# Layernorm by quarters, tiles mixed over pairs and two banks, ternary copies on VectorE

## The chip, the cores and the metric

One Trainium2 chip, one core. The metric is the device time in microseconds of one execution, the median of several runs. Engines are named TensorE (PE, with its weight loads as PEld), VectorE (DVE), ScalarE (ACT), GpSimd (POOL) and SyncE (SP, which here issues every transfer).

## What is computed

One transformer layer in fp32, on x of 8 batches x 1024 rows x 512. First differential attention: layernorm, q, k and v by one 512 x 1536 product, 16 heads of 32; the first 16 dimensions of a head give one softmax and the last 16 another; the second is subtracted with a factor; then a root-mean-square norm per head, and a product with wo. Then a feed-forward part with weights rounded to -1, 0, 1.

```python
qkv = x @ w_qkv                       # x is the layernorm of the input
a1 = softmax(einsum('bhsd,bhtd->bhst', q1, k1) * scale)
a2 = softmax(einsum('bhsd,bhtd->bhst', q2, k2) * scale)
out = einsum('bhst,bhtd->bhsd', a1 - lam * a2, v)
out_n = out / sqrt(mean(out * out) + EPS) * norm_w * (1.0 - LAMBDA_INIT)
x = x + (out_n reshaped) @ wo
h = bitlinear(ln(x), w_fc) + gate * (ln(x) @ v.T @ fast_b.T @ u.T)
x = x + bitlinear(relu(h) ** 2, w_proj)   # bitlinear: ternary weight times a row scale
```

## The kernel before, in words

**Chunks and tiles.** The 8192 rows are 16 chunks of 512 rows (C). A chunk of the input lies in `xin` as four row tiles of 128. Its layernorm is made in steps by `dve_ln_step`: four statistics (L1099), four gathers (L1104), a logarithm and an exponential on ScalarE (`act_ln`, L876 and L878), a correction step (`dve_newton`, L1110 to L1116) and four applies (`dve_apply`, L1121). Then it is turned: TensorE transposes it by column blocks of 128 (`pe_turn`, L479, four transposes each), ScalarE copies the result, rounded, to `xth` (`act_turn`, L884), and VectorE subtracts that for the low half `xtl` (`dve_turn`, L1148). From the turned rows come 12 tiles of a chunk (T, i = T mod 12): eight of q and k (i < 8), each of 12 matmuls (L503), with a copy on ScalarE (L900), a low half (`dve_low`, L1155) and a maximum of magnitudes (`dve_bound`, L1165) on VectorE, and three stores; and four of v (L506), with one ScalarE copy (L905) and no VectorE work.

**Pairs.** Chunks 0 and 1 (batch 0) are made ahead. Then 64 pairs of heads follow, eight in each batch. A pair has 16 slots (k), two in each of 8 steps (d = 0 to 7). A slot has two score halves on TensorE (`pe_score`, L564), two exponentials on ScalarE (`act_exp`, L921, 128x1024 each, 32 in a pair), one add of the probabilities into `acc` on VectorE (`dve_add`, L1222, 128x2048, none at slots 0 and 8), and the product with v (`pe_pv`, L589). The scores use banks 0 to 3, the products 4 and 5. `pe_sum` (L610) sums `acc` over partitions into bank 7, for slots 0 to 7 (j = 0) at step 5, and for 8 to 15 (j = 1) at step 1 of the next pair. ScalarE makes its reciprocal by a logarithm and an exponential (L927, L931).

What follows a pair X is spread over the next three (`*_posts`, d counts on from 8 and 16): combine (L1234, L1237), transpose (`pe_post` 3, L631), copy to `on` (L946), square on GpSimd (L283), sums (L1243), norm (L1248), split (L958, L1252), the product with wo into bank 7 (`pe_post` 14 and 15, L645), the residual on VectorE at d = 16 (L1258), and the store.

**The order** of each engine's instructions is written out by hand in loops over P, d and half; semaphores order the engines. In pair P the tiles 24 + 3P to 26 + 3P are made in pieces of 6, 8 or 4 matmuls at steps 0 to 5 (`PIECES`), all in bank 6: the first matmul of a tile waits, by `tile_read`, until the tile before has been read. Tiles come in the order of i: of four pairs, the first two make three q/k tiles, the third two and a v tile, the fourth three v tiles. All steps of a later chunk's layernorm lie in the first of four pairs and the start of the second (`steps`, `rest`); its four turns are at steps 2 and 6 of the second pair and at step 6 of the third and the fourth (`turn_at`). When the fourth pair's turn is done, SyncE loads the next chunk in one transfer. Pairs 0 to 51 carry layernorm and tiles, 52 to 55 tiles alone.

**The last eight pairs** have no tiles. There the weights are made ternary, one of eight tiles in each pair: magnitudes on ScalarE (L971), scale and comparison on VectorE (L1283 to L1298), four transposes of four blocks each on TensorE into bank 6 (`pe_ternary`, L732, at steps 6, 7, and 0, 1 of the next pair) and their copies on ScalarE (`act_ternary`, L982). In these pairs TensorE adds slots 7 and 15 itself (L618). Behind the loop come factors of the low-rank part, the rest of the last pairs, and the feed-forward part: 16 blocks of 512 rows (L669, L674, L689).

## Time and profile before

| what | us |
|---|---|
| median of 3 runs | 3943.78 (3939.89 to 3952.39) |
| profiled execution | 3940.3 |
| its span | 3938.6 |
| TensorE busy | 3774.7 (96%) |
| VectorE busy | 3205.4 (81%) |
| ScalarE busy | 2782.0 (71%) |
| GpSimd busy | 99.5 (3%) |
| mean granted clock of TensorE | 0.992 |

The span is the time from the first to the last instruction of the profiled execution. Busy time counts instructions in the engine and no waits. A granted clock of 1.00 is 2.4 GHz. In the trace, a wait is written with the one who waited ahead of the arrow and the one who ended it behind. A row of windows gives a stretch of the span, its length, then the busy time (and the number of instructions) of TensorE, its weight loads, VectorE, ScalarE and GpSimd, the granted clock, the share of the transfer engines' time, and GB/s. The stretches are cut at the first exponential (L921) of a pair. A group's row ends with its busy time in all, the mean of one in ns, and the idle time before it.

### The profile page before, as it was taken

The page shows a single profiled execution, that of the slowest core. Times are in us where ns is not written, and L with a number is a line of the kernel's source. Part 1 is how long each engine was busy: PE and PEld are TensorE (multiplying, and loading weights), DVE is VectorE, ACT ScalarE, POOL GpSimd, SP SyncE. Part 2 cuts the span into 40 slices and gives each one's busy share as a digit, 9 for nine tenths or more (in the row PEclk, how much of TensorE's full clock was granted, in tenths as well). Part 3 has the DMA queues.
Part 4 walks back from the last instruction along what each step waited for, and adds up shares of the span by engine and source line. Part 5 has one row for each costly group of instructions (what it writes and reads, how often), then busy time and mean ns, then how long its engine had stood idle before and what let it go on. Part 6 is the DMA issues. An engine that isn't in the chain of part 4 may idle for free.

```text
span 3938.6 us, 57545 instructions
## 1 busy us (share of the span) xinstructions
PE 3774.7 (96%) x21960; PEld 2070.1 (53%) x21960; DVE 3205.4 (81%) x3089; ACT 2782.0 (71%) x3597; POOL 99.5 (3%) x78
## 2 busy tenths in 40 slices
PE   6799999999999999999999999999889999999999
PEld 5344444444444444444444444333378888888887
DVE  5699999999999999999999999988855555555554
ACT  2688888888888888888888888988733333333333
POOL 0000000000000000000000000000000000000000
PEclk9899999999999999999999999999989999999999
DMA  5545444445444445444444445433101010101010
GB/s 196 129 101 114 99 112 108 102 107 111 111 99 114 108 96 121 104 108 104 108 106 107 112 93 115 103 74 90 48 10 43 22 43 22 43 22 43 22 43 22
DMA packets 225844, 338.24 MB, mean 86 GB/s; under 512 B 86704, under 2 KB 107184, under 8 KB 225008
## 3 DMA queue, kind: packets, MB, share of 16 engines
q1 hardware_dynamic: 225520, 333.88, 34.7%
q8 instruction: 208, 3.41, 0.4%
q14 instruction: 116, 0.95, 0.1%
HBM read 180.72 MB, written 150.99 MB: 84 GB/s over the span
## 4 chain that ended last, share of the span: by engine, by line
PE 65%; DVE 22%; ACT 5%; issue 5%; DMA 1%; SPq 1%; DVEq 0%; ACTq 0%
DVE acc L1222 17%; PE ps L589 13%; PE ps L689 12%; PE ps L669 12%; PE ps L564 10%; PE ps L506 5%; PE ps L645 4%; PE ps L503 3%; ACT pr L921 3%; PE ps L610 2%; PE ps L674 1%; DVE stg L1155 1%; PE ps L719 1%; DVE ot L1234 1%; PE ps L709 1%
## 5 line engine op out<-in xcount | busy, mean ns | idle before, releaser
L921 ACT ACTIVATE pr<-ps 128x1024 f32<-128x1024 f32 x2048 | 1989.7, 1032 | 278.4 <-PE ps L564 272.3
L1222 DVE TENSOR_TENSOR acc<-acc,pr 128x2048 f32<-128x2048 f32 x752 | 1736.5, 2309 | 39.5 <-ACT pr L921 16.0
L589 PE MATMUL ps<-pr,vst 128*32 128x512 f32 x8192 | 1023.3, 601 | 0.0
L564 PE MATMUL ps<-qst,kst 50*128 50x512 f32 x4096 | 800.0, 460 | 58.9 <-ACT pr L921 38.0
L564 PEld LDWEIGHTS ps<-qst,kst 50*128 50x128 f32 x4096 | 339.3, 184 | 730.8 <-ACT pr L921 515.5
L1075 ACT ACTIVATE rb<-ps,scf 128x512 f32<-128x512 f32 x256 | 176.7, 690 | 388.4 <-PE ps L674 388.4
L589 PEld LDWEIGHTS ps<-pr,vst 128*32 128x32 f32 x8192 | 208.5, 109 | 429.2 <-issue 423.8
L689 PE MATMUL ps<-tP,hh_ 128*128 128x512 f32 x1024 | 404.4, 395 | 1.9 <-DVE hl_ L1442 1.9
L669 PE MATMUL ps<-yh,tT 128*128 128x512 f32 x1024 | 404.5, 395 | 0.0
L669 PE MATMUL ps<-yl,tT 128*128 128x512 f32 x1024 | 399.5, 390 | 0.0
L689 PE MATMUL ps<-tP,hl_ 128*128 128x512 f32 x1024 | 399.1, 390 | 0.0
L1440 DVE TENSOR_TENSOR sb<-rb 128x512 f32<-128x512 f32 x256 | 176.9, 691 | 268.7 <-ACT rb L1075 267.1
L1222 DVE TENSOR_TENSOR acc<-pr 128x2048 f32<-128x2048 f32 x128 | 292.8, 2288 | 110.4 <-ACT pr L921 109.0
L1442 DVE TENSOR_TENSOR hl_<-sb,hh_ 128x512 fp32r<-128x512 f32 x256 | 177.3, 693 | 179.3 <-ACT hh_ L1080 179.3
L1080 ACT ACTIVATE hh_<-sb 128x512 fp32r<-128x512 f32 x256 | 162.4, 635 | 205.3 <-DVE sb L1440 205.3
L503 PE MATMUL ps<-xth,wqh 128*128 128x512 f32 x512 | 222.1, 434 | 31.3 <-DVE stg L1155 31.3
L689 PEld LDWEIGHTS ps<-tP,hh_ 128*128 128x128 f32 x1024 | 192.1, 188 | 56.8 <-DVE fo L1480 12.6
L669 PEld LDWEIGHTS ps<-yl,tT 128*128 128x128 f32 x1024 | 192.5, 188 | 38.9
L669 PEld LDWEIGHTS ps<-yh,tT 128*128 128x128 f32 x1024 | 192.5, 188 | 38.5
L689 PEld LDWEIGHTS ps<-tP,hl_ 128*128 128x128 f32 x1024 | 192.3, 188 | 37.7
L503 PE MATMUL ps<-xtl,wqh 128*128 128x512 f32 x512 | 206.7, 404 | 0.0
L503 PE MATMUL ps<-xth,wql 128*128 128x512 f32 x512 | 202.3, 395 | 0.0
(154 smaller groups left out, 3493.6 us busy)
## 6 DMA issues: line engine op xcount, KB each, us to landing
qst<-q_scratch SPq DMA_DIRECT2D x128, 384.0 KB, 6.3
kst<-k_scratch SPq DMA_DIRECT2D x128, 384.0 KB, 9.6
q_scratch<-stg SPq DMA_DIRECT2D x168, 256.0 KB
k_scratch<-stg SPq DMA_DIRECT2D x168, 256.0 KB
xin<-in_L_attn_x_dram SPq DMA_DIRECT2D x16, 1024.0 KB, 5.4
v_scratch<-vsg SPq DMA_DIRECT2D x64, 256.0 KB, 3.1
vst<-v_scratch SPq DMA_DIRECT2D x128, 128.0 KB, 5.4
xr<-in_L_attn_x_dram SPq DMA_DIRECT2D x64, 256.0 KB
```

Of the source, the lines that this page charges most:

```text
L503: t = e.matmul(ps[:, bk, :], w[:, k, m0:m0 + 128], xx[:, k, :], start=(n == 0), stop=(n == 11))
L506: t = e.matmul(ps[:, bk, :], xx[:, k, st * 128:(st + 1) * 128], w[:, k, 2 * E:3 * E], start=(n == 0), stop=(n == 11))
L564: ins = e.matmul(ps[:, 2 * c + hh, :], kst[rows, r, j, t * 128:(t + 1) * 128], qst[rows, r, j, c * 512:(c + 1) * 512], start=True, stop=True)
L589: ins = e.matmul(ps[32 * c4:32 * c4 + 32, 4 + j, :], vst[:, r, t, 32 * hh:32 * hh + 32], pr[:, sl, c, hh, :], start=(t == 0), stop=(t == 7 ...
L669: e.matmul(ps[:, bk, :], tT[:, k, i * 128:(i + 1) * 128], y_[:, bf, k, :], start=(m == 0), stop=False)
L689: t = e.matmul(ps[:, rt, :], h_[:, uu % 3, rt * 128:(rt + 1) * 128], tP[:, i, :], start=(i == 0 and part == 0), stop=(i == 15 and part == 1))
L921: e.activation(pr[:, sl, c, :, :], ps[:, 2 * c:2 * c + 2, :], ACT.Exp, scale=SCALE).then_inc(s_exp, 1)
L1075: e.activation(rb[:, uu % 2, :], ps[:, 4 + uu % 2, :], ACT.Relu, scale=scf[:, 0, i:i + 1]) \
L1080: e.activation(hh_[:, uu % 3, :], sb2[:, uu % 2, :], ACT.Copy).then_inc(s_hh, 1)
L1222: e.tensor_tensor(acc[:, j, :], old, new, ALU.add).then_inc(s_add, 1)
L1440: e.tensor_tensor(sb2[:, uu % 2, :], rb[:, uu % 2, :], rb[:, uu % 2, :], ALU.mult).then_inc(s_sb, 1)
L1442: e.tensor_tensor(hl_[:, uu % 3, :], sb2[:, uu % 2, :], hh_[:, uu % 3, :], ALU.subtract) \
```

## The change

- The layernorm of chunks 3 to 15 goes by quarters. Pair P works for chunk C = P // 4 + 3 and row tile st = P mod 4 (`part_of`). VectorE takes one statistic in each pair at step 0 (all four of chunk 3 in pair 0), gathers them in the first of four pairs at step 1 and corrects at step 3. The apply becomes a ScalarE instruction with a scale and a bias per row, one in each pair at step 5. TensorE transposes the four blocks of that row tile at step 6 (`pe_part`), with one copy and one subtraction behind it. Each pair loads one row tile of the next chunk.
- Tiles follow `ORDER`: in an even chunk each pair has two q/k tiles and one v tile, in an odd one the pairs have 2, 3, 3 and 0 q/k tiles. The second tile of each pair goes to bank 7, the others to bank 6 (`TILE_BANK`); the waits follow.
- The square of a pair's result is a ScalarE instruction out of bank 5 (step 4) instead of a GpSimd one.
- The residual (L1258 of before) comes half a step earlier, ahead of the last add.
- The ternary transposes are at steps 0, 2, 3, 4 of the next pair (`TERNARY`), and their copies on VectorE; the last tile's four lie behind the loop.

```diff
+TILE_BANK = (6, 7, 6)
+ORDER = ((0, 1, 8, 2, 3, 9, 4, 5, 10, 6, 7, 11), (0, 1, 8, 2, 3, 4, 5, 6, 7, 9, 10, 11))
+TERNARY = (0, 2, 3, 4)
...
 def turned(P):
-    return min(12 + P // 4 * 4 + (0, 0, 2, 3)[P % 4], 4 * NC)
...
+    return min(12 + P, 4 * NC)
...
-            for X in range(NPAIR):
...
-                e.wait_ge(s_raw, X + 1)
-                if X:
-                    e.wait_ge(s_ssq, X)
-                e.tensor_tensor(sq[:], on[:], on[:], ALU.mult).then_inc(s_osq, 1)
...
+        def sync_part(e, P):
+
+            C, st = part_of(P)
+            e.wait_ge(s_xt, turned(P) + 1)
+            e.dma_start(xin[:, st, :], x_chunk(C + 1)[:, st, :]).then_inc(s_xp[st], 16)
...
-                    if d == 7 and P % 4 == 3 and w + 4 < NC:
-                        sync_x(e, w + 4)
+                    if d == 7 and w + 4 < NC:
+                        sync_part(e, P)
...
+        def pe_part(e, P):
+
+            C, st = part_of(P)
+            e.wait_ge(s_pap, P + 1)
+            e.wait_ge(s_pt, 2 * P + 1)
+            for k in range(4):
+                t = e.transpose(ps[:, 4, k * 128:(k + 1) * 128], xin[:, st, k * 128:(k + 1) * 128], ident[:])
+            t.then_inc(s_xt, 1)
...
                 if j == 0:
                     e.wait_ge(s_xtl, turned(P))
                 elif P:
-                    e.wait_ge(s_raw, P)
+                    e.wait_ge(s_osq, P)
...
                 e.wait_ge(s_rln, 2 * X)
-                e.wait_ge(s_flv, 6 * min((X + 1) // NP + 1, B) - 1)
+                if 3 * X + 24 < 24 * B:
+                    tile_read(e, 3 * X + 25)
...
-                            if T > 24:
+
+                            if a == 1:
+                                e.wait_ge(s_rln, 2 * P)
+                                e.wait_ge(s_flv, 5)
+                                e.wait_ge(s_xtl, 12)
+                            elif a == 2:
+                                tile_read(e, T - 2)
+                                if q == NP - 1:
+                                    e.wait_ge(s_flv, 6 * (P // NP + 1) + 5)
+                            elif P:
                                 tile_read(e, T - 1)
                             else:
                                 e.wait_ge(s_xtl, 12)
-                        pe_tile(e, T, 6, n0, n1)
+                        pe_tile(e, T, TILE_BANK[a], n0, n1)
...
-                    if turn_at(P, d):
-
-                        e.wait_ge(s_pt, 2 * P + (1 if d == 6 else 0))
-                        pe_turn(e, *turn_at(P, d))
+                    if d == 6 and part_of(P):
+                        pe_part(e, P)
                     pe_posts(e, P, d)
-                    if last and d >= 6:
-                        pe_ternary(e, P - (NPAIR - NP), d - 6)
-                    if last and d < 2 and P > NPAIR - NP:
-                        pe_ternary(e, P - (NPAIR - NP) - 1, d + 2)
+                    if P > NPAIR - NP and d in TERNARY:
+                        pe_ternary(e, P - (NPAIR - NP) - 1, TERNARY.index(d))
...
-            pe_pv(e, NSLOT - 2)
-            pe_ternary(e, 7, 2)
-            pe_pv(e, NSLOT - 1)
-            pe_ternary(e, 7, 3)
+            for m in range(4):
+                if m in (0, 2):
+                    pe_pv(e, NSLOT - 2 + m // 2)
+                pe_ternary(e, 7, m)
...
+        def act_part_apply(e, P):
+            st = P % 4
+            e.wait_ge(s_pnv, 9 * (P // 4) + 9)
+            e.activation(xin[:, st, :], xin[:, st, :], ACT.Identity, bias=ln_t[:, 20 + st:21 + st],
+                         scale=rs[:, 8 + st:9 + st]).then_inc(s_pap, 1)
...
+            if d == 4 and half == 1:
+                if X:
+                    e.wait_ge(s_ssq, X)
+                e.activation(sq[:], ps[:, 5, :], ACT.Square).then_inc(s_osq, 1)
...
-                    if P % 4 == 0 and d == 6 and w + 3 < NC:
-                        act_ln(e, w + 3, mv, ln_t, rs)
+                    if d == 2 and P % 4 == 0 and part_of(P):
+                        act_part_ln(e, w)
...
-                        act_tile(e, 24 + 3 * P + d // 2, 6)
-                    if turn_at(P, d):
-                        act_turn(e, *turn_at(P, d))
+                        act_tile(e, 24 + 3 * P + d // 2, TILE_BANK[d // 2])
+                    if d == 5 and part_of(P):
+                        act_part_apply(e, P)
+                    if d == 6 and part_of(P):
+                        act_part(e, P)
...
-                    if d >= 6 and tile >= 0:
-                        act_ternary(e, tile, d - 6)
-                    if d < 2 and tile >= 1:
-                        act_ternary(e, tile - 1, d + 2)
...
-            if d == 16 and half == 0:
+            if d == 15 and half == 2:
...
-            steps = {(1, 1): (0,), (2, 0): (1,), (3, 0): (2,), (4, 0): (3,), (5, 0): (4,), (6, 1): (6,), (7, 0): (7,),
-                     (7, 1): (8,)}
-            rest = {(0, 0): (9,), (0, 1): (10,)}
...
+                        if (d, half) == (0, 1) and P < 4 * (NC - 3) - 3:
+                            dve_part_stats(e, P)
+                        if P % 4 == 0 and part_of(P):
+                            if (d, half) == (1, 0):
+                                dve_part_gather(e, w)
+                            if (d, half) == (3, 1):
+                                dve_part_newton(e, w)
...
+                        if d == 7 and half == 1:
+                            dve_post(e, P - 2, 15, 2)
                         dve_add(e, P, 2 * d + half)
+                        if tile >= 1 and d in TERNARY and half == 1:
+                            dve_turn_ternary(e, tile - 1, TERNARY.index(d))
...
-            dve_post(e, NPAIR - 3, 16, 0)
+            for m in range(4):
+                dve_turn_ternary(e, 7, m)
```

## Rows read from the trace of the kernel before

**Rows 1.** Windows of the run: pairs 0 to 51, 52 to 55, 56 to 63.

```profile
130.10:2331.20 2201.10, 2149.26 (x13700) 953.17 (x13702) 2094.95 (x1585) 1894.30 (x2307) 82.87 (x51) 1.00 0.46 106
2331.20:2495.80 164.60, 163.77 (x1051) 71.84 (x1040) 156.24 (x107) 143.66 (x173) 5.35 (x4) 1.00 0.49 113
2495.80:2838.70 342.90, 309.96 (x2041) 107.52 (x2038) 301.46 (x264) 302.34 (x415) 8.92 (x10) 1.00 0.33 73
```

**Rows 2.** Windows by pair: 20, 21, 22 and 23, then 8 and 12.

```profile
976.05:1018.50 42.45, 40.77 (x264) 17.98 (x260) 41.25 (x41) 36.24 (x47) 2.09 (x1) 1.00 0.48 113
1018.50:1062.15 43.65, 41.86 (x272) 18.83 (x268) 42.90 (x33) 36.86 (x46) 1.04 (x1) 1.00 0.46 110
1062.15:1103.75 41.60, 41.35 (x268) 18.32 (x264) 40.54 (x27) 36.39 (x45) 1.04 (x1) 1.00 0.45 103
1103.75:1145.20 41.45, 41.45 (x272) 18.42 (x268) 37.05 (x29) 36.49 (x46) 2.26 (x1) 1.00 0.46 103
467.70:511.70 44.00, 42.34 (x264) 18.28 (x260) 41.57 (x41) 36.24 (x46) 2.08 (x1) 0.96 0.47 109
638.10:680.70 42.60, 40.94 (x264) 17.98 (x260) 41.37 (x41) 36.36 (x47) 2.07 (x1) 1.00 0.48 113
```

**Rows 3.** Waits in pair 20, pair 21 (two) and pair 22: us in total, times, longest.

```profile
PE ps L503 <- DVE stg L1155: 1.7, 1, 1.7
...
PE ps L610 <- DVE xr L1258: 1.0, 1, 1.0
PE ps L503 <- DVE stg L1155: 0.8, 2, 0.4
...
ACT pr L921 <- PE ps L564: 4.9, 9, 0.8
```

**Rows 4.** Groups of the whole run; then single lines with ns min/median/max.

```profile
L1222 DVE TENSOR_TENSOR acc<-acc,pr 128x2048 f32<-128x2048 f32 x752 | 1736.5, 2309 | 39.5 <-ACT pr L921 16.0 <-DVE acc L1222 1.0
L1075 ACT ACTIVATE rb<-ps,scf 128x512 f32<-128x512 f32 x256 | 176.7, 690 | 388.4 <-PE ps L674 388.4
L931 ACT ACTIVATE rl<-rl 128x512 f32<-128x512 f32 x128 | 81.2, 634 | 4.1
L1155 DVE TENSOR_TENSOR stg<-ps,stg 128x512 fp32r<-128x512 f32 x112 | 76.5, 683 | 0.0
L1472 DVE CAST zt<-ps 32x512 fp32r<-32x512 f32 x16 | 11.1, 697 | 0.5
...
L1222 DVE TENSOR_TENSOR acc<-acc,pr x752: 2215/2286/2903, 138.7 to 2837.2; 128x2048 f32<-128x2048 f32 x188
...
L283 POOL TENSOR_TENSOR sq<-on x64: 1038/1041/3062, 194.5 to 2862.3; 128x512 f32<-128x512 f32 x64
...
L1099 DVE BATCH_NORM_STATS2 st<-xin x64: 675/684/694, 9.9 to 2189.4; 128x6 f32<-128x512 f32 x64
L1121 DVE TENSOR_SCALAR xin<-xin,mv,rs x64: 529/540/547, 26.3 to 2211.3; 128x512 f32<-128x512 f32 x64
...
L982 ACT ACTIVATE tP<-ps x16: 580/600/628, 2702.2 to 2842.1; 128x512 fp32r<-128x512 f32 x16
```

**Rows 5.** Pair 58: its window, and waits in it.

```profile
2580.70:2623.70 43.00, 38.95 (x260) 13.56 (x256) 37.22 (x31) 37.89 (x53) 1.04 (x1) 1.00 0.36 81
...
DVE acc L1222 <- ACT pr L921: 3.4, 2, 3.2
ACT tT L982 <- PE ps L732: 2.8, 2, 1.8
ACT rl L927 <- PE ps L618: 2.0, 2, 1.5
```

**Rows 6.** Transfers; VectorE's timeline behind the loop; ScalarE's at the start.

```profile
xin<-in_L_attn_x_dram SPq DMA_DIRECT2D x16, 1024.0 KB, 5.4
...
2855.58 0.75 DVE L1258 SCALAR_TENSOR_TENSOR xr<-ps,nw,xr 128x512 f32<-128x512 f32 x1 [5.40 <-DMA xr<-in_L_attn_x_dram]
...
0.80 1.28 ACT L1001 ACT_TABLE_LOAD   x1 [0.80 <-PEq L1506]
```

More of the change, by code:

```diff
@@ L209, in build @@
         s_lnv, s_lna = sem("s_lnv"), sem("s_lna")
+        s_pst, s_pnv, s_pap, s_pta = (sem(n) for n in ("s_pst", "s_pnv", "s_pap", "s_pta"))
+        s_xp = [sem(f"s_xp{k}") for k in range(4)]
         s_xt, s_xth, s_xtl, s_tile, s_qh, s_ql, s_qx, s_v, s_flv, s_flp = (
@@ L496, in pe_tile @@
                 k, part = divmod(n, 3)
-                if i == 0 and part == 0:
+                if i == 0 and part == 0 and C < 3:
                     e.wait_ge(s_xtl, 4 * C + k + 1)
+                elif i == 0 and n == 0:
+                    e.wait_ge(s_xtl, 4 * C + 4)
                 w = (wqh, wql, wqh)[part]
@@ L610, in pe_sum @@
                     t = e.matmul(ps[32 * c4:32 * c4 + 32, bk, :], ones[:], acc[:, j, (2 * c + hh) * 512:(2 * c + hh + 1) * 512],
[L611 to L612 removed]
+                                 start=True, stop=not pe_adds(X, j), skip_group_check=True)
+            if pe_adds(X, j):
                 gg = 16 * X + 8 * j + 7
@@ L1370, in vector_program @@
                     for half in range(2):
-                        if half == 1 and turn_at(P, d):
-                            dve_turn(e, *turn_at(P, d))
+                        if (d, half) == (6, 1) and part_of(P):
+                            dve_turn_part(e, P)
                         if d == 5 and half == 0:
```

171 lines of the change are left out of this document (103 added, 68 removed).

## The prediction, made before the changed kernel was built or run

> **What bounds the kernel now.** I read the stages first, cut at the first exponential of pairs 0, 52, 56 and behind 63 [rows 1]: 52 pairs that still make q, k and v tiles take 2201.1 us (42.33 each), four that make tiles but have no layernorm left take 164.6 (41.15 each), the last eight, which turn ternary weights instead, 342.9 (42.9 each). The feed-forward part behind them is not touched. In the first stage TensorE is busy 2149.3 of 2201.1 us: it is the bound, and 51.8 us are gaps. Next, one group of four pairs [rows 2]: 42.45, 43.65, 41.60 and 41.45 us, TensorE busy in 40.77, 41.86, 41.35 and 41.45 of them. So a pair with one turn of rows (268 matmuls) needs 41.35 us; one with none (264) 0.6 less, one with two (272) 0.5 more. The gaps, 3.7 us in four pairs, lie in the first two, where VectorE is fullest (41.25 and 42.90 us; 37.05 in the fourth). Then who ends the gaps [rows 3]: a q or k tile's first matmul waits 1.7 and 0.8 us for L1155, VectorE's low half of the tile before, because every tile uses bank 6, and the row sums L610 wait 1.0 us for L1258, which empties bank 7. VectorE is late there, not full on average: it is busy 161.74 of 169.15 us.
>
> A second thing comes on top of such gaps: pair 8 takes 44.0 us at a granted clock of 0.96, pair 12, with the same work, 42.6 at 1.00 [rows 2]. At the halved clock (1.2 GHz instead of 2.4) stands a short stretch of the slow pair. I count four of these (pairs 4, 8, 36 and 40, about 1.5 us each, 6 us together), all in a pair that begins with the 1.7 us gap.
>
> The last eight pairs are another case: in pair 58 [rows 5] ScalarE is busy 37.89 us and waits 2.8 us for L732, the ternary transposes, and 2.0 for the row sums: 42.7 of 43.0. It is the bound; TensorE needs 38.95, VectorE 37.22.
>
> **The change, part by part**, against the profiled execution: 3940.3 us, of which the span is 3938.6; the median of the three runs, 3943.8, is 3.5 above it.
>
> Layernorm. Four applies (L1121, 0.540 us each) leave VectorE per four pairs, one small instruction comes, so 2.0 us less per four pairs. The four statistics, 0.684 each, stay, but lie one in each pair instead of four in the first. ScalarE gets one apply per pair with a scale and a bias from memory. No row shows that form. SBUF to SBUF without pointers takes 0.634 us (L931); a pointer scale adds 0.09 (L1075, 0.690, beside 0.600 of L982, both out of PSUM) [rows 4]. I take 0.81 with two pointers, between 0.63 and 0.90. For this the trace has a contrary number: it was 0.54 on VectorE. In a sentence of its own: the Trainium skill, "ScalarE: Activation LUTs", Rules for kernel authors, tells to do adds and multiplies on VectorE, not on ScalarE; by that rule the step is a loss of 0.27 us of engine time per apply, which would count only if ScalarE were the bound, and that is the third rival.
>
> Squares. GpSimd's product (L283, 1.04 us alone, up to 3.06) becomes a ScalarE instruction out of PSUM, 0.60 us by L982. VectorE gains what the overlap cost it: the 752 long adds average 2.309 us where the median is 2.286 [rows 4], 17 us in all, 0.27 a pair. In sentences of their own: the Trainium skill, "SBUF — State Buffer", Who interferes with whom, says that the pair of ports which the two engines share is locked and the loser waits in full; each product would then cost VectorE up to 1.04 us, 66 us in all, and removing it would be worth four times as much. The median and the mean above show that most products cost nothing, and I keep 17.
>
> So VectorE's load in four pairs goes from 161.7 to 161.7 - 2.0 - 1.1 = 158.6 us, 39.7 a pair against 41.35 of TensorE.
>
> Tiles. In groups with an even chunk every pair now has two q/k tiles, each with L1155 (0.68 us) and a reduction of the same length, and one v tile, which needs no VectorE; in the odd groups the counts are 2, 3, 3, 0. The middle tile goes to bank 7, between the row sums of j = 1 and those of j = 0, so the third tile waits for the first, two steps back, not for the one before. This takes away the place of the 1.7 and 0.8 us waits. L1258 moves half a step earlier, in front of the last add; both stand ahead of the row sums either way, so only the lighter VectorE helps there. The nearest rows for the new state are pairs 52 to 55: three q/k tiles, one bank, no layernorm, and gaps of 164.6 - 163.8 = 0.8 us in four pairs [rows 1]. The new plain pair has as many VectorE instructions (two tiles, a statistic and a subtraction of a turn instead of a third tile), the first of each group has nine small ones more, the odd groups' middle pairs two long ones more. I leave 12 us of VectorE gaps in 52 pairs (0.2 each as there; bounds 0 and half of the present 52).
>
> ScalarE. Per pair it gets 0.60 (square, step 4) and 0.81 (apply, step 5), 1.41 beside 36.4 busy of 42. In pair 22 it waits for scores nine times, 4.9 us, 0.8 at most [rows 3]. The square finds such a wait just behind it; the apply stands behind a logarithm, an exponential and a tile copy, where there is none, and its 0.81 must go into the waits of the next step, of which some 0.6 is free. I take 0.2 us a pair on the path, 10 us; the bounds are 0 and all of the 1.41, 73 us.
>
> DMA. SyncE issues 52 loads of 256 KB instead of 13 of 1 MB. A load starts when TensorE has turned its quarter at step 6, behind the v load on the queue, and the statistic that needs it comes at step 0 of the next pair, two steps (some 10 us) later; 1 MB lands in 5.4 us [rows 6], so I cost it at nothing. Were this cover gone, VectorE would stand in order for up to 5 us a pair with its adds behind. The transposes of a quarter at step 6 wait for the apply of step 5 and free bank 4 as before; their count is the same.
>
> First stage: 51.8 - 12 - 10 = 30 us, plus 5 of the 6 us of halved clock, because the gap ahead of those stretches goes: **35 us** less.
>
> Ternary copies. From ScalarE go four copies (2.4 us) and the 2.8 us of waits for their transposes, and 0.6 comes: 38.3 us. VectorE gets four copies out of PSUM, 0.697 by L1472 [rows 4]: 37.2 + 2.8 = 40.0, and of its 3.4 us of waits for exponentials [rows 5] at least 0.8 stays: 40.8. So VectorE becomes the bound: 2.2 us less in seven pairs, 0.5 in pair 56, **16 us** (bounds: 0 where TensorE's transposes wait for late copies, and 28 at 39.4 us a pair, TensorE's need with half a microsecond of gap).
>
> End. Two more ternary pieces lie behind the loop, each a transpose and a copy in turn, about 1.5 us. They hide beneath two transfers, after which L1258 waits another 5.40 us [rows 6]. Without that cover 3 us; I take **1 us** more.
>
> Sum: 3940.3 - 35 - 16 + 1 = 3890 us. Another execution may lie a few microseconds to either side, as the median of before does; I add nothing for it.
>
> **The rivals.** (a) Everything at TensorE's floor: gaps and dips nearly all gone (54 us) and 39.7 us in the last pairs (26): 3860. For it: pair 23 has no gap at all. Against: no ScalarE room at step 5. (b) The waits move on to the row sums and to late exponentials, a third of the first stage's gain and 5 us at the end stay: 3940 - 15 - 5 = 3920. For it: L610 already waits for L1258 [rows 3]. (c) Slower: ScalarE becomes the path at steps 4 and 5. Its waits are short ones between scores; if none takes the 1.41 us, every exponential behind it, and with it the score and the add that wait for it, comes that much later, the present gaps stay, and only the 16 us of the end are won: 3940 + 73 - 16 = 3997. It decides once more than about 1.2 us a pair is on the path (35 + 10 + 16 over 52). (d) The new functions need another table than the one loaded at the start. The trace shows one such load, 1.28 us [rows 6]; there and back once a pair would be 2.6 us in 64 pairs: 3890 + 164 = 4054. The Trainium skill, "ScalarE: Activation LUTs", Table sets, says that the cheap functions are filler in every set; its examples have identity, not square. That the change doesn't do what it says is a variant of (b): the stages keep their order, and only the load moves.
>
> **How the numbers follow.** Forecast, 3872 to 3908, 0.62; (a) 0.14; (b) 0.15; (c) 0.06; (d) 0.03. The range leaves out (c), (d) and the far parts of (a) and (b): 3860 to 3925. What a measurement here tells from no change is 0.3%, 12 us; (b) reaches into that a little. Faster 0.88, same 0.04, slower 0.08.
>
> **What would show it.** Right: pairs 0 to 51 near 41.7 us with hardly a wait on L1155's counterpart; no short stretches at half clock inside them; last pairs near 40.8 with VectorE above 39.5 and ScalarE waiting for scores; long adds with mean equal to median. Wrong: first-stage pairs still above 42; exponentials 11 to 13 of each pair late with TensorE idle ahead of a score; table loads inside the pairs; VectorE idle for a quarter's load at the start of a pair.

## The result, and the profile after

The changed kernel takes 3922.69 us (median of five runs, 3919.04 to 3923.53), the kernel before 3943.78 (3938.83 to 3952.39): a ratio of 0.9942 (0.9927 to 0.9958). That is faster by 21 us, where 50 had been forecast: the right side, inside the outer range (3860 to 3925) but outside the forecast's own (3872 to 3908), and less than half of the size. The profiled execution after took 3922.69 us, its span 3920.9. Against the span of before that is 17.7 us, and the rest of this text accounts for them.

Windows of the kernel after, cut at the same first exponentials as in [rows 1]: pairs 0 to 51, 52 to 55, 56 to 63, and what lies behind. Columns: length, then busy time of TensorE, its weight loads, VectorE, ScalarE and GpSimd, then the granted clock, the DMA share and GB/s.

```profile
131.50:2304.10 2172.60, 2152.33 (x13700) 954.40 (x13702) 2067.74 (x1542) 1946.65 (x2411) 0.00 (x0) 1.00 0.47 108
2304.10:2467.50 163.40, 163.40 (x1048) 71.92 (x1040) 154.39 (x107) 144.98 (x177) 0.67 (x2) 1.00 0.48 114
2467.50:2818.30 350.80, 309.50 (x2032) 105.19 (x2030) 311.15 (x292) 293.30 (x393) 0.00 (x0) 0.99 0.32 71
2818.30:3920.90 1102.60, 1080.16 (x4852) 877.48 (x4844) 594.63 (x1026) 408.69 (x654) 0.20 (x1) 0.99 0.10 32
```

| us | up to pair 0 | 0 to 51 | 52 to 55 | 56 to 63 | behind | span |
|---|---|---|---|---|---|---|
| before | 130.1 | 2201.1 | 164.6 | 342.9 | 1099.9 | 3938.6 |
| after | 131.5 | 2172.6 | 163.4 | 350.8 | 1102.6 | 3920.9 |
| difference | +1.4 | -28.5 | -1.2 | +7.9 | +2.7 | -17.7 |
| forecast | 0 | -35 | 0 | -16 | +1 | -50 |

The forecast is off by 32 us of span. Of these 24 are in the last eight pairs, which became 7.9 us longer instead of 16 shorter, and 6.5 in the first stage. The 1.4 us ahead of pair 0 mean nothing: that stretch takes 129.9 to 131.9 us in the kernels of this text. The 1.2 us in pairs 52 to 55 go with the second bank: the kernels with one bank take 164.4 there (experiments 5 and 10), the others 163.4 to 163.5. Nothing in the last eight pairs was slowed by more work on a full engine. VectorE is busy 311.15 of 350.80 us, ScalarE 293.30, TensorE 309.50; all three have more than 39 us to spare.

Windows by pair after: 20, 21, 22, 23 (their counterparts are the first four of [rows 2]), and pair 58 (before: [rows 5]).

```profile
966.97:1009.14 42.17, 41.62 (x268) 18.35 (x264) 40.60 (x37) 37.78 (x49) 0.00 (x0) 1.00 0.46 108
1009.14:1050.74 41.60, 41.37 (x268) 18.45 (x264) 39.97 (x30) 37.40 (x47) 0.00 (x0) 1.00 0.53 122
1050.74:1092.39 41.65, 41.43 (x268) 18.45 (x264) 40.75 (x30) 37.40 (x48) 0.00 (x0) 1.00 0.51 121
1092.39:1134.27 41.88, 41.66 (x272) 18.48 (x268) 38.82 (x30) 37.50 (x48) 0.00 (x0) 1.00 0.41 84
2552.23:2596.02 43.79, 38.47 (x260) 13.27 (x256) 38.69 (x35) 36.60 (x50) 0.00 (x0) 1.00 0.35 80
```

The four pairs of a group are nearly level now: 42.17, 41.60, 41.65 and 41.88 where they had been 42.45, 43.65, 41.60 and 41.45. The 1.7 and 0.8 us waits for a tile's low half [rows 3] are gone. In pairs 3 to 51 there is no stretch at half clock any more, where there were four. Near the start of the stage one is left, in pair 1; before, it was in pair 2. The groups that answer to [rows 4], ns per instruction behind the comma:

```profile
L1296 DVE TENSOR_TENSOR acc<-acc,pr 128x2048 f32<-128x2048 f32 x752 | 1719.9, 2287 | 50.3 <-ACT pr L965 18.6
...
L919 ACT ACTIVATE xin<-xin,ln_t,rs 128x512 f32<-128x512 f32 x52 | 42.3, 813 | 0.0
...
L994 ACT ACTIVATE sq<-ps 128x512 f32<-128x512 f32 x64 | 39.0, 609 | 0.0
...
L751 PE MATMUL ps<-ident,tt 128*128 128x128 f32 x128 | 21.5, 293 | 15.9 <-DVE tP L1384 9.1 <-DVE tT L1384 6.8
...
L1384 DVE CAST tT<-ps 128x512 fp32r<-128x512 f32 x16 | 10.9, 684 | 0.0
```

Every duration of the prediction holds: the long adds mean 2287 ns where 2286 was the median before, the apply takes 813 ns (0.81), the square 609 (0.60), the copy on VectorE 684 (0.697). What was wrong lies in how they join, and the fourth row shows it: TensorE's ternary transposes (L751) now wait 15.9 us for the copies, 12.5 of them in pairs 57 to 63 and the rest behind the loop.

Pair 58 after, the longest waits and then its timeline from 12.3 us into the pair (start, duration, engine, line; in brackets the idle time before it and what ended that):

```profile
ACT pr L965 <- PE ps L583: 6.9, 6, 1.9
DVE acc L1296 <- ACT pr L965: 4.0, 3, 2.1
...
ACT rl L971 <- PE ps L638: 2.0, 2, 1.0
PE ps L751 <- DVE tT L1384: 1.7, 1, 1.7
```

```profile
2564.51 7.08 DVE L1296 TENSOR_TENSOR acc<-acc,pr 128x2048 f32<-128x2048 f32 x3
...
2569.98 0.66 PE L650 MATMUL ps<-ident,ot 128*128 128x128 f32 x4
...
2571.51 0.69 DVE L1384 CAST tT<-ps 128x512 fp32r<-128x512 f32 x1
...
2572.34 0.63 PE L751 MATMUL ps<-ident,tt 128*128 128x128 f32 x4 [1.70 <-DVE tT L1384]
...
2573.44 1.94 ACT L965 ACTIVATE pr<-ps 128x1024 f32<-128x1024 f32 x2 [1.89 <-PE ps L583]
```

Read it from below. ScalarE stands idle 1.89 us for a score; the score is behind the third piece's transposes (L751) on TensorE; these need bank 6, which the copy of the second piece (L1384) empties; and that copy is on VectorE behind three adds in a row, 7.08 us. The same chain is in each of the seven pairs 57 to 63; TensorE's wait is 1.70 us in six of them and 2.30 in pair 62. Three pairs lose more behind it, in a stretch where TensorE is at half its clock: pairs 57, 58, 60 and 63 take 43.8 to 43.9 us, pair 59 takes 44.7, pair 61 44.6 and pair 62, with its longer wait, 45.3. One such stretch, in pair 59:

```profile
2617.00:2620.40 3.40, 3.40 (x16) 0.81 (x14) 3.33 (x9) 2.43 (x3) 0.00 (x0) 0.53 0.02 5
```

The longer wait, in pair 62:

```profile
2749.79 0.97 PE L751 MATMUL ps<-ident,tt 128*128 128x128 f32 x4 [2.30 <-DVE tP L1384]
```

In the stretch of pair 59 eight products of probabilities take 1.93 us, where eight take 1.06 elsewhere in these pairs.

### The profile page after: what moved, and what is told of

It is laid out like the page before. It is cut to its first block, busy times and chain, and to the rows that moved or that the text cites. A ratio compares the mean times of both kernels' runs of the same rounds, so it can differ in the third digit from the quotient of the medians.

```text
span 3920.9 us, 57542 instructions
## 1 busy us (share of the span) xinstructions
PE 3780.6 (96%) x21960; PEld 2070.3 (53%) x21960; DVE 3191.6 (81%) x3082; ACT 2824.7 (72%) x3681; POOL 2.0 (0%) x14
## 4 chain that ended last, share of the span: by engine, by line
PE 77%; ACT 9%; DVE 8%; issue 4%; SPq 1%; DMA 1%; DVEq 0%; ACTq 0%
PE ps L608 17%; PE ps L583 13%; PE ps L708 12%; PE ps L688 12%; PE ps L521 8%; DVE acc L1296 6%; ACT pr L965 5%; PE ps L664 5%; PE ps L630 3%; PE ps L524 3%; PE ps L693 1%; ACT rl L971 1%; ACT rl L975 1%; ACT xin L919 1%; PE ps L738 1%
## 5 line engine op out<-in xcount | busy, mean ns | idle before, releaser
L965 ACT ACTIVATE pr<-ps 128x1024 f32<-128x1024 f32 x2048 | 1982.0, 1030 | 265.5 <-PE ps L583 259.5
L1296 DVE TENSOR_TENSOR acc<-acc,pr 128x2048 f32<-128x2048 f32 x752 | 1719.9, 2287 | 50.3 <-ACT pr L965 18.6
L583 PE MATMUL ps<-qst,kst 50*128 50x512 f32 x4096 | 809.5, 462 | 65.5 <-ACT pr L965 44.6
```

What stands on the lines that cost most here:

```text
L583: ins = e.matmul(ps[:, 2 * c + hh, :], kst[rows, r, j, t * 128:(t + 1) * 128], qst[rows, r, j, c * 512:(c + 1) * 512], start=True, stop=True)
L965: e.activation(pr[:, sl, c, :, :], ps[:, 2 * c:2 * c + 2, :], ACT.Exp, scale=SCALE).then_inc(s_exp, 1)
L1296: e.tensor_tensor(acc[:, j, :], old, new, ALU.add).then_inc(s_add, 1)
```

## The experiments

Two questions: why the last pairs became longer, and what the parts of the first stage are worth. Each kernel is the changed one with the edit shown, if nothing else is said. Stages are from each kernel's profile, ratios against the kernel before on the same chip.

How far a stage repeats can be read from kernels whose code in pairs 0 to 51 is the same: the changed one and experiments 1, 2 and 11 take 2172.6, 2170.4, 2174.0 and 2172.5 us there. All of that scatter is in the first four pairs, where none, one or two stretches at half clock come. Pairs 4 to 51 have none in any kernel but the one before, so they are the better measure for small effects (worked out from the starts of the pairs' first exponentials):

| us | pairs 0 to 3 | stretches there | pairs 4 to 51 |
|---|---|---|---|
| before | 167.0 | 1 | 2034.2 (with four stretches) |
| after | 167.0 | 1 | 2005.6 |
| 1, 2, 11 | 164.8, 168.6, 166.9 | 0, 2, 1 | 2005.6, 2005.4, 2005.6 |
| 3: square on GpSimd | 168.6 | 2 | 2008.7 |
| 4: apply on VectorE | 164.0 | 0 | 1982.9 |
| 5: one bank | 165.5 | 0 | 2018.1 |
| 6: unmixed | 166.8 | 1 | 2005.9 |
| 8 | 163.7 | 0 | 1983.0 |
| 9: correction late | 166.0 | 1 | 1976.4 |
| 10: spreading alone | 166.1 | 1 | 2006.4 |

The windows of pairs 4 to 51 before, after and in experiment 4:

```profile
297.05:2331.23 2034.18, 1989.35 (x12700) 883.73 (x12696) 1942.94 (x1477) 1751.52 (x2137) 76.63 (x48) 1.00 0.46 107
298.47:2304.08 2005.61, 1990.33 (x12700) 884.49 (x12696) 1917.25 (x1438) 1800.45 (x2234) 0.00 (x0) 1.00 0.47 108
294.73:2277.59 1982.86, 1978.50 (x12700) 882.31 (x12696) 1926.90 (x1486) 1767.35 (x2186) 0.00 (x0) 1.00 0.48 110
```

**1. The end as before.** Places, bank and engine of the ternary copies as in the kernel before; the rest of the change stays.

```diff
-                    if P > NPAIR - NP and d in TERNARY:
-                        pe_ternary(e, P - (NPAIR - NP) - 1, TERNARY.index(d))
+                    if last and d >= 6:
+                        pe_ternary(e, P - (NPAIR - NP), d - 6)
+                    if last and d < 2 and P > NPAIR - NP:
+                        pe_ternary(e, P - (NPAIR - NP) - 1, d + 2)
...
+                    if d >= 6 and tile >= 0:
+                        act_ternary(e, tile, d - 6)
+                    if d < 2 and tile >= 1:
+                        act_ternary(e, tile - 1, d + 2)
```

> The changed kernel with the ternary transposes and copies put back: transposes at steps 6, 7, 0, 1, copies on ScalarE. Theory A (the last eight pairs were never bound by ScalarE's load: the 2.8 us that it waited for the ternary transposes were TensorE's queue, and the new order adds a wait of 1.7 us for a copy behind VectorE's adds): last eight pairs 346 us (343 of before plus 0.5 a pair for the square), against 350.8 changed; whole 3917. Theory B (ScalarE's load was the bound there, and something else, such as the square, costs the gain): moving 2.4 us a pair back to ScalarE makes the last eight pairs longer, 360 or more; whole 3932.

Measured 3909.82 us, ratio 0.9918 (0.99 to 0.9935). The last eight pairs are back at their length, what lies behind them takes 1100.0 us, and no stretch at half clock is left in the pairs:

```profile
2464.40:2807.00 342.60, 309.99 (x2038) 107.77 (x2038) 296.12 (x264) 305.78 (x423) 0.00 (x0) 1.00 0.33 73
```

So this part of the change costs 8.2 us in the pairs and 2.6 behind them; in pairs 0 to 3 this execution is 2.2 us shorter besides, with no stretch at half clock there. Theory B falls. It also says that the square, 0.6 us on ScalarE in each of these pairs, costs nothing here, where 0.5 had been expected: 342.6 with it and 342.9 without.

**2. The third piece in bank 7.** Places and engine as in the change; only the bank of one piece in four differs, so that its transposes do not wait for the second piece's copy.

```diff
+def ternary_bank(i, m):
+    return 7 if i < 7 and m == 2 else 6
...
-            if u4:
+            if i < 7 and m == 2:
+                e.wait_ge(s_rln, 2 * (NPAIR - NP + i + 1))
+            elif i < 7 and m == 3:
+                e.wait_ge(s_tt, u4 - 1)
+            elif u4:
```

> The changed kernel with the third ternary transpose of a tile in bank 7, so that it does not wait for the copy of the second. Theory A (one wait for a bank): the 1.7 us wait at step 3 goes in seven pairs (12 us), and with it the three short stretches of halved clock behind it (2.5 us): last eight pairs 336 us, whole 3908. Theory C (VectorE's load, not the bank, holds the last pairs): the wait moves to the next place that needs VectorE, last eight pairs 347 or more, whole 3919 or more.

Measured 3903.86 us, ratio 0.99 (0.9883 to 0.9918). Windows of pair 58 and of the last eight pairs, then pair 58's longest waits of ScalarE:

```profile
2550.83:2592.72 41.89, 38.26 (x260) 13.31 (x256) 38.69 (x35) 36.61 (x51) 0.00 (x0) 1.00 0.37 84
2468.00:2802.30 334.30, 304.40 (x2034) 104.81 (x2030) 310.92 (x292) 292.81 (x393) 0.00 (x0) 1.00 0.33 75
```

```profile
ACT pr L975 <- PE ps L587: 5.0, 5, 1.8
...
ACT rl L981 <- PE ps L644: 2.0, 2, 1.0
```

One bank is worth 16.5 us: 350.8 becomes 334.3. Seven pairs have 41.9 to 42.0 us each, the wait of 1.70 us (2.30 in pair 62) is gone in all of them, and with it the three stretches at half clock. Without that wait this part of the change, new places and copies on VectorE together, gives 8.3 us against experiment 1 (342.6), half of the 16 forecast.

**3. The square back on GpSimd.**

```diff
+                e.wait_ge(s_raw, X + 1)
+                if X:
+                    e.wait_ge(s_ssq, X)
+                e.tensor_tensor(sq[:], on[:], on[:], ALU.mult).then_inc(s_osq, 1)
...
-                e.activation(sq[:], ps[:, 5, :], ACT.Square).then_inc(s_osq, 1)
```

> The changed kernel with the square back on GpSimd. Theory A: in pairs 0 to 51 the square falls into a wait of ScalarE and costs nothing, in the last eight it costs 0.5 us each: pairs 0 to 51 within 3 us of 2172.6, last eight 347, whole 3919; long adds of VectorE at a mean of 2.31 again. Theory D (every ScalarE instruction in steps 4 to 6 is on the path): 0.6 us less in each of 60 pairs, whole 3887.

Measured 3925.32 us, ratio 0.9958 (0.9943 to 0.9974), the first stage 2177.3 us against 2172.6, the last pairs 349.9.

```profile
L1301 DVE TENSOR_TENSOR acc<-acc,pr 128x2048 f32<-128x2048 f32 x752 | 1739.4, 2313 | 43.7 <-ACT pr L974 7.2
...
L293 POOL TENSOR_TENSOR sq<-on 128x512 f32<-128x512 f32 x64 | 80.1, 1252 | 2727.5 <-ACT on L999 2727.5
```

The long adds are back at 2313 ns, 26 more than after, or 19.5 us of VectorE's time in the run. Of the 4.7 us in the first stage 3.1 are in pairs 4 to 51, nearly all of them in the first pair of each group (42.4 us against 42.2); the rest is in pairs 0 to 3, with one more stretch at half clock. The last pairs are 0.9 us shorter because two of them have such a stretch and not three; without one they take 43.8 us as after. So ScalarE's path is no shorter without the square, and theory D falls. The whole is 2.6 us above the changed kernel, and the runs of the two overlap.

**4. The apply back on VectorE**, still one quarter a pair, right ahead of the add of step 4's second half.

```diff
-                    if d == 5 and part_of(P):
-                        act_part_apply(e, P)
...
+                        if (d, half) == (4, 1) and part_of(P):
+                            dve_part_apply(e, P)
```

> The changed kernel with the quarter's apply on VectorE (0.54 us, one in each pair, at step 4) instead of ScalarE. Theory A (ScalarE has no room at step 5; VectorE has 1.5 us a pair to spare): step 5 about 0.7 us shorter, step 6 0.3 longer, 0.4 us less in each of 52 pairs, 20 us in all: pairs 0 to 51 2152 us, whole 3902. Theory E (VectorE's late adds hold the row sums as soon as anything is added): the 0.54 us come back as waits of the row sums at step 5, pairs 0 to 51 2170 us or more, whole 3920 or more.

Measured 3898.23 us, ratio 0.9892 (0.9872 to 0.9912). The first stage, and pair 21:

```profile
130.80:2277.60 2146.80, 2137.15 (x13700) 951.84 (x13702) 2078.15 (x1594) 1911.03 (x2359) 0.00 (x0) 1.00 0.48 109
997.25:1038.37 41.12, 41.12 (x268) 18.42 (x264) 40.29 (x31) 36.70 (x46) 0.00 (x0) 1.00 0.51 123
```

25.8 us less in 52 pairs, and 22.7 in pairs 4 to 51, 0.47 each (the other 3.0 us are in pairs 0 to 3, where this execution has no stretch at half clock and the changed kernel's has one). ScalarE had been busy only 37.4 of 41.6 us, and still 0.5 of the 0.81 us lay on the path. Only this place on ScalarE was tried: whether the apply would have been free at another step of it is open. Look at TensorE too: the same 268 matmuls are busy 41.12 us here and 41.37 after, so half of the loss hid inside TensorE's busy time.

**5. All tiles in bank 6**, the row sums alone in bank 7.

```diff
-TILE_BANK = (6, 7, 6)
+TILE_BANK = (6, 6, 6)
```

> The changed kernel with all q, k and v tiles in bank 6 again (order of the tiles, layernorm by quarters and the last pairs as changed). Theory A (the second bank takes away a wait for the low half wherever a q or k tile follows one): about 0.3 to 0.5 us of gap in most of pairs 0 to 51, these 2190 us, whole 3940 beside 3922.7. Rival F (spreading layernorm and tiles already lets VectorE be in time, the bank gives nothing): pairs 0 to 51 within 3 us of 2172.6.

Measured 3936.45 us, ratio 0.9986 (0.9976 to 0.9996). The first stage, and from the waits of pair 9 those for the low half L1220:

```profile
130.70:2314.35 2183.65, 2149.63 (x13700) 951.92 (x13702) 2067.60 (x1542) 1951.20 (x2410) 0.00 (x0) 1.00 0.46 107
```

```profile
PEld ps L524 <- DVE stg L1220: 0.7, 1, 0.7
PEld ps L521 <- DVE stg L1220: 0.4, 1, 0.4
...
PE ps L524 <- DVE stg L1220: 0.3, 1, 0.3
```

The second bank is worth 11.1 us of the first stage, 12.5 in pairs 4 to 51, somewhat less than the 17 expected: TensorE's wait that comes back is 0.3 us (0.7 for its weight load), not the 1.7 of [rows 3]. That fits VectorE's work being spread now; it was not tried apart. (This kernel's profiled run, 3932.88 us, is the shortest of its ten.)

**6. Tiles not mixed**: eight q and k tiles, then four v tiles, over the two banks.

```diff
-ORDER = ((0, 1, 8, 2, 3, 9, 4, 5, 10, 6, 7, 11), (0, 1, 8, 2, 3, 4, 5, 6, 7, 9, 10, 11))
+ORDER = (tuple(range(12)), tuple(range(12)))
```

> The changed kernel with the tiles of a chunk in their old order (3, 3, 2, 0 q/k tiles in four pairs), two banks kept. Theory A (with two banks only the row sums wait for VectorE, and layernorm is spread): the first of each four pairs about 0.5 us longer, the rest as changed, pairs 0 to 51 2180 us, whole 3930. Rival G (the mix of tiles is what removed the gaps): pairs 0 to 51 2195 us or more, whole 3945.

Measured 3920.74 us, ratio 0.9951 (0.9934 to 0.9968), the first stage 2172.63 us against 2172.60, and pairs 4 to 51 2005.9 against 2005.6. With two banks the mix gives nothing. The expectation of a loss falls.

**7. Edits 2 and 4 together.**

> The third ternary transpose in bank 7 and the apply on VectorE together. Theory A (the two costs lie in different stages and add): pairs 0 to 51 2147 us, last eight 334, whole about 3880. Rival H (the second gain is limited by something that the first left): less than 35 us of gain over the changed kernel, whole 3888 or more.

Measured 3880.3 us, ratio 0.9845 (0.9823 to 0.9867): the first stage 2148.8, the last pairs 334.4. The two gains add up, as they should if they lie in different stages.

**8. Besides, the last tile's four copies alternate between banks 6 and 4** behind the loop, where the change has bank 6 four times in turn.

```diff
+    if i == 7:
+        return 4 if m % 2 else 6
```

> As the one before, and the four transposes behind the loop alternate between banks 6 and 4. Theory A (the end is longer by 2.8 us since those transposes and copies take turns, and the product behind them then runs at half the clock): the stretch behind pair 63 comes back to 1100 us or a little less, whole 3 us less than the one before. Rival I (two transfers in a row set that stretch, as before): no difference within 1 us.

Measured 3877.8 us, ratio 0.9843 (0.9821 to 0.9865). What lies behind the loop is 1101.1 us against 1102.9 in experiment 7: 1.8 less, and in the medians not to be told from nothing.

**9. Besides, the small instructions of the layernorm** in the first pair of a group half a step later: behind the add that the row sums of step 5 wait for, not ahead of it.

```diff
+                        if (d, half) == (4, 0) and P % 4 == 0 and part_of(P):
+                            dve_part_newton(e, w)
...
-                            if (d, half) == (3, 1):
-                                dve_part_newton(e, w)
```

> As x8 (third ternary transpose in bank 7, apply on VectorE, two banks behind the loop), with the correction of the layernorm in the first of four pairs half a step later, behind the add of slot 7 instead of in front of it. Theory A (the first of four pairs is 0.5 us longer because the row sums at step 5 wait for that add): 41.2 instead of 41.7 us in 13 pairs, pairs 0 to 51 2140 us, whole 3872. Rival J (the 0.5 us is something else of that pair, such as ScalarE's logarithm and exponential at step 2): no difference beyond 1 us.

Measured 3874.08 us, ratio 0.9838 (0.9824 to 0.9852), the fastest here. Its first stage, pair 20 (the first of its group), and its last pairs:

```profile
130.75:2273.20 2142.45, 2137.55 (x13700) 949.72 (x13702) 2076.65 (x1594) 1911.64 (x2358) 0.00 (x0) 1.00 0.47 109
955.60:996.72 41.12, 41.12 (x268) 18.37 (x264) 39.97 (x38) 37.10 (x49) 0.00 (x0) 1.00 0.50 111
2436.60:2770.90 334.30, 304.24 (x2030) 104.57 (x2030) 310.76 (x292) 292.93 (x393) 0.00 (x0) 1.00 0.34 74
```

The first pair of a group now takes 41.12 us with TensorE busy in all of it, and the stage 4.3 us less than in experiment 8 (2146.8), close to what was expected. In pairs 4 to 51 it is 6.6 us, 0.55 in each of twelve groups; a stretch at half clock in pair 1, which experiment 8 does not have, hides the rest. The whole first stage is shorter than TensorE's busy time in it before (2149.26 [rows 1], some of it at half clock).

**10. The spreading alone**: statistics, apply and load by quarters, the apply on VectorE; the square on GpSimd, one bank, tiles unmixed and the end as before.

> Only the spreading of layernorm over the pairs is left of the change: apply on VectorE, square on GpSimd, one bank, old order of tiles, last eight pairs as before. Theory A (the parts add up: spreading alone takes away some 40 of the 51.8 us of gaps, the second bank another 11, and the apply on ScalarE gave 26 back): pairs 0 to 51 2160 us, last eight 343, whole 3900. Rival K (spreading needs the lighter VectorE of the other parts): pairs 0 to 51 2175 us or more, whole 3915 or more.

Measured 3912.79 us, ratio 0.9934 (0.9918 to 0.995), the first stage:

```profile
129.86:2302.34 2172.48, 2144.74 (x13700) 946.13 (x13702) 2107.77 (x1594) 1892.47 (x2308) 69.93 (x51) 1.00 0.47 108
```

This lies between the two expectations and nearer to the second, that the banks and the square have a share of their own. The spreading alone takes 28.6 us off the first stage of before, just what the whole change takes off. The second bank, the square and the mix together take another 25.7 (the first stage of experiment 4 is this plus those three), and the apply on ScalarE gives the same 25.8 back; in pairs 4 to 51 the two are 23.5 and 22.7. Taken out one by one of the changed kernel the same three are worth 12.5, 3.1 and 0.2 there (experiments 5, 3 and 6), 15.8 together: they are worth more beside an apply on VectorE. No run shows why. The median, 3912.79 us, is likewise below the 3922.69 of the whole change. One pair of the last eight took 44.1 us in this run, with a stretch at half clock in it; the pairs beside it took 42.9 to 43.1, and the reading does not rest on it.

**11. The copies on VectorE, everything else of the end as before**: the old steps 6, 7, 0 and 1, each copy ahead of the add of its half step.

```diff
+                        if tile >= 0 and d >= 6 and half == 1:
+                            dve_turn_ternary(e, tile, d - 6)
+                        if tile >= 1 and d < 2 and half == 1:
+                            dve_turn_ternary(e, tile - 1, d + 2)
```

> The ternary transposes at their old steps (6, 7, 0, 1) as in x1, but their copies on VectorE, ahead of the add of the same half step. So ScalarE loses 2.4 us a pair and TensorE's order does not change. Theory A (at steps 6 and 7 ScalarE waits for a score that TensorE has queued behind the product with wo and the transpose; the wait only changes the instruction that it is written on): steps 6 and 7 stay at 6.0 us, only step 0 may lose up to 0.5: last eight pairs 339 to 343 us. Theory B, the one of the prediction (ScalarE is the bound in these pairs, its waits for the transposes go with the copies): 2.4 to 5.2 us less a pair, last eight pairs 326 us or less.

Measured 3913.86 us, ratio 0.9928 (0.9908 to 0.9947); the last eight pairs take 345.9 us, 3.3 more than in experiment 1, where ScalarE copies in the same places. That is the test of the step on which the 16 us had stood: theory B is off by 20 us, and theory A, right in kind, by 3 (its range ended at 343). ScalarE's waits in pair 58 with the copies on ScalarE (experiment 1):

```profile
ACT tT L1032 <- PE ps L751: 2.8, 2, 1.8
ACT rl L973 <- PE ps L638: 1.5, 2, 1.0
ACT pr L967 <- PE ps L583: 0.2, 1, 0.2
```

and with the copies on VectorE (experiment 11), with the pair's window ahead:

```profile
2551.21:2594.64 43.43, 38.78 (x260) 13.48 (x256) 38.78 (x35) 36.58 (x50) 0.00 (x0) 1.00 0.36 81
```

```profile
ACT pr L967 <- PE ps L583: 6.9, 6, 2.2
...
ACT rl L973 <- PE ps L638: 2.1, 2, 1.0
```

The 2.8 us of waits for the transposes are gone by name only. ScalarE does 1.7 us less (36.58, and 38.27 in experiment 1), and its exponentials wait 6.9 us for scores instead of 0.2. Pair 58's window in experiment 1:

```profile
2549.20:2592.10 42.90, 38.88 (x260) 13.58 (x256) 36.35 (x31) 38.27 (x54) 0.00 (x0) 1.00 0.36 82
```

## Why the prediction was wrong, and where it was right

Steps of pair 58, from the first exponential of each step to that of the next, worked out from the starts of L965 or its counterpart (a tile's four pieces lie at steps 6, 7, 0 and 1 in the first three kernels, at 0, 2, 3 and 4 in the last two):

```
us                                    0     1     2     3     4     5     6     7    pair
before                              5.23  5.93  4.23  4.85  4.09  6.54  6.07  6.04  43.0
1: end as before                    5.22  5.93  4.22  4.84  4.57  6.07  6.05  6.04  42.9
11: old places, copies on VectorE   5.50  5.93  4.57  4.84  4.57  6.03  6.00  6.00  43.4
after                               4.75  5.92  4.57  6.89  4.57  5.98  5.56  5.56  43.8
2: third piece in bank 7            4.75  5.91  4.57  5.00  4.57  5.99  5.55  5.55  41.9
```

**The step that failed: "From ScalarE go four copies (2.4 us) and the 2.8 us of waits for their transposes ... So VectorE becomes the bound: 2.2 us less in seven pairs".** It read a full engine out of busy time plus waits: 37.89 busy, 2.8 and 2.0 of waits, 42.7 of 43.0 [rows 5]. Two things were wrong with that. (VectorE's load came out lower too, 38.69 us where 40.0 had been summed: the copies added 2.3 us to it, and without the product on GpSimd its small instructions took 0.9 less. ScalarE's 38.3 are 38.1 by the terms given.)

First, a wait is not work that leaves with the instruction that waits. The two waits of before, 1.05 us in step 6 and 1.78 in step 7, were for TensorE's queue: at these steps the product with wo stands in it ahead of the transposes and ahead of the next scores. With the copies gone from ScalarE, the exponential behind them waits instead, 1.48 and 2.22 us in experiment 11, and still 1.03 and 1.78 after, where no transposes are left in steps 6 and 7 at all. In the table the columns 6 and 7 fall by 0.05 us at most when the copies change their engine, and by half a microsecond each when the transposes leave TensorE's queue there. The Trainium skill, "PSUM — Partial Sum Buffer", Engine vs sequencer instructions, says that matmuls start and complete in program order; so a wait for a matmul lasts until what stands ahead of it in the queue is done. The table agrees. Columns 6 and 7 together give 0.9 us a pair for the new places of the pieces (experiment 2 against 11); the copies on VectorE in the old places give nothing and cost 3.3 us (experiment 11 against 1). The fourth combination, new places with the copies on ScalarE, was not run, so how much of the 8.3 us needs VectorE is open.

Second, the change put the second and third pieces into neighbouring steps with one bank, and their copy onto an engine that has up to three adds of 2.29 us ahead of it. Column 3 is where it shows: 6.89 us against 5.00 with another bank. The prediction had this as its lower bound ("0 where TensorE's transposes wait for late copies"); it lay at zero, and measured it was +8, for it took the wait to eat a gain and not to stand beside a gain that was not there. Worked out: 1.9 us in seven pairs are 13.2, the longer wait of pair 62 is 0.6 and the three stretches at half clock behind these waits some 2.6, 16.4 together, of the 16.5 that the bank gives back in experiment 2.

Without the wait the term is 8.3 us (experiments 1 and 2), not 16: the pair stands at 41.9, not 40.8. Which engine holds it there was not tried; VectorE is busy 38.69 of 41.89 us and ScalarE 36.61, so neither is full.

**The end, +1 forecast, +2.7 measured.** Right in kind. Behind the loop four transposes and four copies take turns in one bank. VectorE's timeline there, and one row of TensorE's:

```profile
2823.24 0.69 DVE L1384 CAST tP<-ps 128x512 fp32r<-128x512 f32 x1 [1.27 <-PE ps L751]
2825.70 0.69 DVE L1384 CAST tP<-ps 128x512 fp32r<-128x512 f32 x1 [1.76 <-PE ps L751]
...
2835.75 0.42 DVE L1496 COPY ut<-ps 128x256 f32<-128x256 f32 x1 [5.69 <-PE ps L638]
...
2838.37 0.74 DVE L1332 SCALAR_TENSOR_TENSOR xr<-ps,nw,xr 128x512 f32<-128x512 f32 x1
```

```profile
2822.12 1.08 PE L751 MATMUL ps<-ident,tt 128*128 128x128 f32 x4 [2.47 <-DVE tP L1384]
```

The cover named was the transfer for which the residual behind the loop waited 5.40 us [rows 6]. Its counterpart, L1332, now waits for nothing and starts 20.1 us behind the end of the last exponential, where it was 16.9, and VectorE waits 5.69 us for TensorE instead: the cover was used up, and TensorE's chain of transposes, wo product and sums became the path. Seven of the wo product's twelve matmuls take 0.63 us or more, at half clock; before, all but the first took 0.39 or 0.40.

**The first stage, 35 forecast, 28.5 measured.** The mechanism was right, the sizes were not, and that the total came near is in part luck: the apply cost 16 us more than its term, and the other two terms came out 10 better:

| term, us | forecast | measured | by |
|---|---|---|---|
| the stage without the two below | 2149.3 - 5 = 2144.3 | 2142.5 | experiment 9 |
| ScalarE's apply on the path | 10 | 25.8 | experiment 4 |
| VectorE's gaps left | 12 | 4.3 | experiments 8 and 9 |
| sum | 2166.3 | 2172.6 | |

In pairs 4 to 51, free of stretches at half clock in these kernels, the apply costs 22.7 us and the gaps are 6.6: the apply was taken at less than half, whichever is used.

- The apply. Its duration was right (0.81 forecast, 813 ns measured) and so was its place: "a logarithm, an exponential and a tile copy" ahead of it, and no wait. Step 5 of pair 22 takes 6.38 us after and 5.69 in experiment 4; step 6 gives back 0.31 (4.97 and 5.28), and step 7 loses 0.13 again. "Of which some 0.6 is free" was the mis-sized part: half of that came back, and no more. That the score which ScalarE waits for there stands in TensorE's queue, held up by the late exponentials, would explain it; that was argued and not tried. For the rule of the Trainium skill, "ScalarE: Activation LUTs", Rules for kernel authors, to leave adds and multiplies to VectorE, this is the measured case: 0.54 us there [rows 4] against 0.81 here, and 23 to 26 us of 3900 for it, though ScalarE was not the bound by its busy time.
- VectorE. The waits for the low half went, as forecast. (The term of 12 us was summed loosely: 0.2 in each of 52 pairs are 10.4.) What stayed is in the first pair of a group, where the row sums of step 5 waited for an add with the small instructions ahead of it; experiment 9 removed it.
- The squares. The overlap with GpSimd cost VectorE what the mean and the median of [rows 4] said, 17 us forecast and 19.5 measured (experiment 3), and 3.1 to 4.7 us of the length. The 66 us of the price by a full lock fell, but so did "most products cost nothing": with 64 products 40 adds take over 2.4 us before and 35 in experiment 3, up to 2.90, and none after, where the longest takes 2.30. ScalarE's 0.6 us for it cost nothing in either stage.
- The tiles. Two banks give 11.1 us (12.5 in pairs 4 to 51), the mix none; the forecast had not told the two apart.
- The half clock. The four stretches behind the 1.7 us waits went with the waits (which lie some 22 us into a pair, not at its beginning as the prediction has it). The prediction overlooked a fifth, in pair 2, behind gaps of 0.65 and 0.51 us; none, one or two such stretches came near the start in kernels with the same code there (table ahead of experiment 1).
- Loads by quarters: in the pairs no statistic waits for one (there are 48 of them, not 52), as forecast. No table is loaded in the pairs.

**The rivals.** (a), all at TensorE's floor, 3860: experiment 9 comes to 3874 with two repairs, so the floor was rightly seen and the change alone could not reach it. (b), part of the gain kept, 3920: its number is 2.7 us off, and by luck. It has 15 us won in the first stage and 5 at the end, and what came is 28.5 won there and 7.9 lost in the last pairs, from a wait for a bank that it does not name. (c), ScalarE as the path: 0.5 us a pair of the 1.41, all of it from the apply; the mechanism is real, its price a third. (d), table loads: none.

## What to carry to other kernels

A wait of engine X for engine Y, where Y works through a queue, belongs to what stands ahead in Y's queue; taking the waiting instruction away from X leaves the wait to the next one. Before calling an engine the bound by "busy plus waits", ask of each wait whether it would go. When a PSUM bank's copy moves to an engine with long instructions, count how many of these can stand ahead of it and give the next user of the bank another bank: here that was worth 16.5 us, twice what the moved pieces give without the wait (8.3). And small work put between two instructions of a chain that has no slack at that place can cost more than half of its length (0.5 of 0.81 us), even on an engine that is a tenth idle.

## What the runs showed of the hardware

- TensorE's busy time is no floor: the same 13700 matmuls of the first stage were busy 2152.33 us after and 2137.55 in experiment 9, 0.7% less, at a granted clock of 1.00 in both. In pair 21 the busy time is 41.37 and 41.12 us for the same 268 matmuls, with and without the apply on ScalarE.
- The half clock follows a wait of about 1.7 us on TensorE, but not each time. Before, twelve pairs have such a gap (1.66 to 1.68 us, some 22 us behind their first exponential) and four of them have the stretch; after, it is in three of the seven pairs with the wait of 1.70 us or more, in experiments 3, 5 and 6 in two, in experiment 4 in three. Removing the wait removed these stretches both times. It is not the only way there: near the start of the first stage, and once in pair 56 (experiment 10), a stretch came behind gaps of 0.4 to 0.9 us.
- A GpSimd product of 1.04 us beside the long adds of VectorE lengthens some of them, to 2.90 us at most where they take 2.29: 17 to 19 us in all for 64 products. Without the products no add takes more than 2.30.
- A total can hide a part that should be undone. Spreading alone is worth 28.6 us, the whole change 28.5, because one part (the apply on ScalarE) takes back just what three others give. And parts need not add: those three are worth 15.8 us one by one and 23.5 together.
